# Constant products in the expert stage's waits, results added one instruction at a time, one normalisation moved to ScalarE, and Newton chains of 11 operations

## The reference

```python
h = take(weight, x)                                  # token rows
h = h + linear_attention(layernorm(h))               # layer 0: relu(q), relu(k), groups of 512 tokens
h = h + expert_choice_ffn(layernorm(h))              # layer 0: 32 experts, each takes its 512 best tokens
h = h + causal_attention(layernorm(h))               # layer 1: 64 batches of 256 tokens, 8 heads of width 128
h = h + top2_ffn(layernorm(h))                       # layer 1: 8 experts, 2 for each token

def expert_choice_ffn(xf):                           # 16384 x 128
    S = softmax(xf @ W_router + b_router)
    G, idx = top_k(S.T, 512)                         # for each of 32 experts
    up = silu(xf[idx] @ W_up[group] + b_up)          # 341 wide
    out = G * (up @ W_down + b_down)
    return zeros.at[idx].add(out)
```

## Time and profile before

| | us |
|---|---|
| median of 3 runs (2581.69 to 2586.2) | 2584.89 |
| the profiled execution | 2591.4 |
| its span in the profile | 2589.7 |

### The profile page before, as it was taken

How to read it: one execution, slowest core, us unless ns; L and a number is a source line. 1 busy time by engine, 2 the same in 40 slices (tenths; PEclk the granted TensorE clock), 3 DMA queues, 4 the chain that set the end, 5 groups by cost and what they waited for, 6 DMA issues and landing times.

```text
span 2589.7 us, 59542 instructions
## 1 busy us (share of the span) xinstructions
PE 2264.2 (87%) x16671; PEld 1982.4 (77%) x16687; DVE 1896.1 (73%) x8436; ACT 1686.8 (65%) x5272; POOL 1473.5 (57%) x1870
## 2 busy tenths in 40 slices
PE   4988978576776899999999999999999999999954
PEld 4877756344443788988888899999998888988854
DVE  4877756656663688888888887887788888888622
ACT  3777744122222777777777788888887777777643
POOL 6444200467766578788888864444444665366553
PEclk9999989789888999999999999999999999999987
DMA  2666630244444611111111146566546776476687
GB/s 73 212 229 205 222 121 1 83 138 142 140 135 131 138 42 42 46 45 49 47 44 46 43 135 171 161 163 172 165 134 187 222 217 198 128 227 196 174 254 241
DMA packets 343687, 357.42 MB, mean 138 GB/s; under 512 B 36491, under 2 KB 285931, under 8 KB 343360
## 3 DMA queue, kind: packets, MB, share of 16 engines
q1 hardware_dynamic: 305856, 265.69, 35.9%
q0 software_dynamic: 34048, 80.03, 9.5%
q10 hardware_dynamic: 3456, 7.89, 1.0%
HBM read 211.02 MB, written 136.67 MB: 134 GB/s over the span
## 4 chain that ended last, share of the span: by engine, by line
PE 54%; DVE 22%; DMA 7%; issue 7%; POOL 4%; ACT 3%; SPq 2%; ACTq 0%; DVEq 0%; POOLq 0%
PE bank L2068 6%; PE bank L2158 6%; PE bank L2144 5%; PE bank L2079 4%; PE bank L2024 4%; PE bank L2111 4%; PE bank L2119 3%; PE bank L2067 3%; PE bank L2091 3%; PE bank L2093 3%; PE bank L2092 3%; PE bank L2037 3%; DVE pr_place L1577 2%; DMA rows<-table,idx 2%; DVE nmax L1557 2%
## 5 line engine op out<-in xcount | busy, mean ns | idle before, releaser
L881 POOL DMA_INDIRECT zbuf<-pc,kb x248 | 250.4, 1010 | 272.8 <-DVE pc L1742 221.9
L866 POOL DMA_INDIRECT spread_rows<-kb,pos x256 | 256.1, 1000 | 171.3 <-DVE pc L1742 81.0
L1081 ACT ACTIVATE pr_place<-bank,nmax 128x128 f32<-128x128 f32 x512 | 188.5, 368 | 223.6 <-DVE nmax L1557 223.5
L2068 PE MATMUL bank<-xT,gT 128*128 128x256 f32 x1024 | 307.4, 382 | 0.0
L1577 DVE COPY pr_place<-bank 128x384 f32<-128x384 f32 x512 | 280.6, 548 | 9.2 <-PE bank L2079 7.8
L2158 PE MATMUL bank<-wvo_part,x_part 128*128 128x512 f32 x768 | 269.3, 459 | 0.0
L2079 PE MATMUL bank<-ident,pr_place 128*128 128x128 f32 x1536 | 252.3, 273 | 17.2 <-DVE pr_place L1577 17.0
L1556 DVE TENSOR_REDUCE nmax<-bank 128x1 f32<-128x128 f32 x512 | 142.9, 279 | 169.1 <-PE bank L2068 167.2
L1091 ACT ACTIVATE bank<-causal 128x384 f32<-128x384 f32 x512 | 253.4, 495 | 19.5 <-PE bank L2202 3.3
L2079 PEld LDWEIGHTS bank<-ident,pr_place 128*128 128x128 f32 x1536 | 195.4, 140 | 87.1 <-DVE pr_place L1570 22.1
L2144 PE MATMUL bank<-x_part,wqk_part 128*128 128x256 f32 x1536 | 245.6, 296 | 1.2 <-DVE x_part L1684 1.2
(11 more groups left out here) (338 smaller groups left out, 6472.9 us busy)
## 6 DMA issues: line engine op xcount, KB each, us to landing
pa<-bundle SPq DMA_DIRECT2D x198, 321.0 KB
table<-rows SPq DMA_DIRECT2D x96, 576.0 KB, 7.0
rows<-table SPq DMA_DIRECT2D x192, 128.0 KB
wu_more<-bundle SPq DMA_DIRECT2D x66, 321.0 KB
junk<-zbuf SPq DMA_DIRECT2D x32, 512.0 KB
kb<-spread_rows SPq DMA_DIRECT2D x248, 65.0 KB
h3buf<-h SPq DMA_DIRECT2D x64, 128.0 KB
kb<-kb SPq DMA_DIRECT2D x32, 256.0 KB
```

The costliest lines, as they stand in the source:

```text
L866: pool.indirect_dma_start(out=spread_rows, out_offset=bass.IndirectOffsetOnAxis(ap=pos[:, k, j:j + 1], axis=0), in_=xr4s[g % 2][:, k, j], ...
L2068: pe.matmul(s2[:, P:3 * P], g[:, P:2 * P], xT3[:, p], start=False, stop=True, skip_group_check=True)\
```

## The change

Four edits. (1) `turn_rows` begins with six constant products into bank 0, ahead of its wait for the gather, and after it two more into bank 3 stand ahead of the wait for `xeT`. (2) `add_rows` and `add_residual` take one tile at a time: `adding` puts one instruction near the start of GpSimd's slot and one at its end, so that the two sums of a result take four slots and not two. (3) `prep_norm` is two ScalarE instructions (`Identity` with a scale and a bias for each row) in slot 4, behind the copy of `gT`; VectorE makes the bias (`prep_shift`, a 128x2 instruction, slot 3). A semaphore that this needed was freed (`b1_ready`: SP's `make_bundle` now waits for `xeT_ready`, which comes later on the same engine). (4) `inv_sqrt` has 11 operations: the factor -0.5 goes into the first, and the constant of the second is adapted. Every one of them now waits for the one before; earlier the third waited for nothing.

```diff
+            def stay_warm(b, times):
+                for _ in range(times):
+                    pe.matmul(bank[b][:, :], slot16[:, 0:P], slot16[:], start=True, stop=True)
+
             def turn_rows(e):
+                stay_warm(0, 6)
                 pe.wait_ge(xe_in[e % 2], 64 * (e // 2 + 1))
...
                     turn_rows(e)
+                    stay_warm(3, 2)
                     pe.wait_ge(xeT_ready, e + 1)
...
-            def add_rows(c):
-                pool.wait_ge(z_in[c % 2], 32 * (c // 2 + 1))
...
+            def adding(u, later):
+                for d in range(2):
+                    if u - 2 - d in RESULT_AT and u - d < U:
+                        add_rows(RESULT_AT[u - 2 - d], 2 * d + later)
+                    if u - 4 - d in RESULT_AT and u - 2 - d < U:
+                        add_residual(RESULT_AT[u - 4 - d], 2 * d + later)
...
+                adding(u, 0)
                 if gated(i - 2) and i <= NG and 1 <= h <= TG:
...
-                if u - 2 in RESULT_AT and u < U:
-                    add_rows(RESULT_AT[u - 2])
-                if u - 3 in RESULT_AT and u <= U:
-                    add_residual(RESULT_AT[u - 3])
+                adding(u, 1)
...
+            def prep_norm(n, p):
+                act.wait_ge(prep_ready, n + 1)
+                if n > 0:
+                    act.wait_ge(xT3_mm, n)
+                for j in range(2):
+                    ins = act.activation(xn3[:, j], hx[:, p, j], ACT.Identity, bias=nm3[:, j:j + 1], scale=r3[:, 0, j:j + 1])
+                ins.then_inc(xn3_ready, 1)
...
+                        if h == 4 and n + 1 < NB:
+                            prep_norm(n + 1, 1 - p)
                         if h == 5 and n + 1 < NB:
                             turned(n + 1, 1 - p)
...
-                if k != 2:
-                    steps.wait()
+                steps.wait()
                 if k == 0:
-                    ins = dve.tensor_scalar(h, v, EPS, None, ALU.add)
+                    ins = dve.tensor_scalar(h, v, EPS, -0.5, ALU.add, ALU.mult)
...
-                elif k == 2:
-                    ins = dve.tensor_scalar(h, h, -0.5, None, ALU.mult)
+                elif k % 3 == 2:
+                    ins = dve.tensor_tensor(t, y, y, ALU.mult)
...
-            def prep_norm(n, p):
+            def prep_shift(n):
                 prep_now["steps"].wait()
-                    ins = dve.tensor_scalar(xn3[:, j], hx[:, p, j], mv3[:, j, 0:1], r3[:, 0, j:j + 1], ALU.subtract, ALU.mult)
+                dve.scalar_tensor_tensor(out=nm3[:], in0=mv3[:, :, 0], scalar=-1.0, in1=r3[:, 0], op0=ALU.mult, op1=ALU.mult)\
+                    .then_inc(prep_ready, 1)
```

More of the change, by code:

```diff
@@ L1 @@
 from contextlib import ExitStack
+from functools import partial
 import concourse.bass as bass
@@ L243, in lm_tower @@
         r3 = sb("r3", [P, 3, 2])
+        nm3 = sb("nm3", [P, 2])
         xn3 = sb("xn3", [P, 2, C])
@@ L451, in lm_tower @@
         consts4 = sem("consts4")
-        b1_ready = sem("b1_ready")
+        prep_ready = sem("prep_ready")
         d_step = sem("d_step")
@@ L640, in make_bundle @@
                 sp.wait_ge(w_c, 16 * (12 + NK))
-                sp.wait_ge(b1_ready, 1)
+                sp.wait_ge(xeT_ready, 1)
                 place = bundle.rearrange("x p c -> p x c")
@@ L883, in give_unit, with add_rows, add_residual @@
                     bounds_check=2 * NTOK - 1, oob_is_err=False).then_inc(z_out[t % YR], 16)
-            def add_rows(c):
-                pool.wait_ge(z_in[c % 2], 32 * (c // 2 + 1))
[L887 to L897, removed]
+            def add_rows(c, j):
+                if j == 0:
+                    pool.wait_ge(z_in[c % 2], 32 * (c // 2 + 1))
+                    if c >= 2:
+                        pool.wait_ge(out_done[c % 2], 16 * (c // 2))
+                ins = pool.tensor_tensor(res[:, c % 2, j], zx[:, c % 2, j, 0:C], zx[:, c % 2, j, C:2 * C], ALU.add)
+                if j == TG - 1:
+                    ins.then_inc(res_step, 1)
+            def add_residual(c, j):
+                if j == 0:
+                    pool.wait_ge(res_step, c + 1)
+                ins = pool.tensor_tensor(res[:, c % 2, j], res[:, c % 2, j], h3x[:, c % 2, j], ALU.add)
+                if j == TG - 1:
+                    ins.then_inc(res_ready, 1)
             def normalise(u, h):
@@ L1040, in _ @@
                     act.wait_ge(bup_mm, 2)
-                    act.activation(b1T[:].rearrange("p x k -> p k x"), bank[2][:, 0:2 * E1].rearrange("p (k x) -> p k x", k=2), ACT.Copy).then_inc(b1_ready, 1)
+                    act.activation(b1T[:].rearrange("p x k -> p k x"), bank[2][:, 0:2 * E1].rearrange("p (k x) -> p k x", k=2), ACT.Copy)
             act.wait_ge(bup_ready, 2)
@@ L1098, in _ @@
                 set_mask(u)
+            prep_norm(0, 0)
             turned(0, 0)
@@ L1205, in _ @@
             assert bias.n == BIAS_STEPS
[L1207 removed]
+            ROOT = 11
             def inv_sqrt(k, steps, v, y, t, h):
[L1211 to L1212 removed]
+                steps.wait()
                 if k == 0:
[L1214 removed]
+                    ins = dve.tensor_scalar(h, v, EPS, -0.5, ALU.add, ALU.mult)
                 elif k == 1:
[L1216 to L1218 removed]
+                    ins = dve.tensor_scalar(y.bitcast(I32), h.bitcast(I32), -0.5, float(0x5F3759DF - (1 << 30) - (1 << 22)), ALU.mult, ALU.add)
+                elif k % 3 == 2:
+                    ins = dve.tensor_tensor(t, y, y, ALU.mult)
                 elif k % 3 == 0:
[L1220 to L1221 removed]
                     ins = dve.tensor_tensor(t, t, h, ALU.mult)
@@ L1539, in prep_stats, with prep_root @@
                 n_.wait()
-            def prep_root(k):
+            def prep_root(n, k):
+                if k == 0 and n > 0:
+                    dve.wait_ge(xn3_ready, n)
                 if k < ROOT:
                     inv_sqrt(k, prep_now["steps"], mv3[:, :, 1], r3[:, 0], r3[:, 1], r3[:, 2])
-            def prep_norm(n, p):
+            def prep_shift(n):
                 prep_now["steps"].wait()
-                if not first(n):
-                    dve.wait_ge(xT3_mm, n)
-                for j in range(2):
-                    ins = dve.tensor_scalar(xn3[:, j], hx[:, p, j], mv3[:, j, 0:1], r3[:, 0, j:j + 1], ALU.subtract, ALU.mult)
-                ins.then_inc(xn3_ready, 1)
+                dve.scalar_tensor_tensor(out=nm3[:], in0=mv3[:, :, 0], scalar=-1.0, in1=r3[:, 0], op0=ALU.mult, op1=ALU.mult)\
+                    .then_inc(prep_ready, 1)
             def maxima(u, h):
@@ L1690, in _ @@
             for k in range(ROOT):
-                prep_root(k)
-            prep_norm(0, 0)
+                prep_root(0, k)
+            prep_shift(0)
             assert prep_now["steps"].n == PREP
@@ L1762, in slots @@
                         if h in (1, 2, 3) and n + 1 < NB:
-                            root = [prep_root, 5 * (h - 1), 1, 1]
+                            root = [partial(prep_root, n + 1), 5 * (h - 1), 1, 1]
                         elif p == 0 and h in (6, 7) and gated(i - 1):
@@ L1799, in slots @@
                         if h == 3 and n + 1 < NB:
-                            prep_norm(n + 1, 1 - p)
+                            prep_shift(n + 1)
                         if h == 6 and n + 1 < NB:
```

## The result

| | us |
|---|---|
| median of 5 runs (2564.35 to 2569.22) | 2568.23 |
| before beside it, median of 5 runs | 2586.2 |
| ratio, 95% interval | 0.9927 [0.9909, 0.9945] |
| span of the profiled execution (before 2589.7) | 2566.5 |

A forecast was written before the change was run, and what follows sets the result against it. Late gathers and TensorE's lowered clock were taken to bound the expert stage, TensorE itself 1500 to 1900 us. Terms -23.4 - 9 + 3 + 1 = -28.4 us gave 2556.5 us, range 2545 to 2573.

The forecast's parts named there:

- Constant products: Expert stage: eight products per expert fill TensorE's waits and hold its clock; -23.4 us, bounds 0 and -25.
- waits for the gather stay under 1 us: Expert stage, profile after: TensorE's waits for each expert's gathered rows were to be shorter than 1 us.
- I take 0: First expert: six products at half speed cost 2.6 us and may give back 1.8 + 0.9; net put at 0.
- Rival (a): Expert stage: the clock holds only in part, so half of the 23.4 us comes; 2568 us, chance 0.15.
- (e): Expert stage: products run, but the clock falls during the rest of the gather wait; 2580 us, chance 0.04.
- Spread sums: Late layer 1: shorter runs of GpSimd's sums cut TensorE's waits for VectorE's copy and clock falls; -9 us, bounds 0 and -14.
- The step that sized a wait by GpSimd's run: Late layer 1: VectorE waits out GpSimd's unbroken run of sums; six 2.54 us, four 1.7, two 0.85.
- Rival (b): Late layer 1: the lock goes by single instructions, the gate's list makes the waits; -9 falls away, 2565.5 us, chance 0.10.
- ScalarE: Layer 1 batches: normalisation moved to ScalarE delays TensorE's transposes 0.05 to 0.2 us; +3 us, range 0 to +12.
- (c): Layer 1: ScalarE carries the moved work half visibly, 0.3 us for 63 batches; +16, 2572 us, chance 0.08.
- (d): TensorE's full stretch: ScalarE's 0.87 us per batch lie fully ahead of the exponentials; slower, 2608 us, chance 0.03.
- Newton chains: Inverse roots: less VectorE issue, but one operation moves ahead of the copy in the gate's first slot; +1 us, -2 to +4.

## Why the prediction was right, and where it was off

**Constant products: right.** -23.4 was forecast; with this edit alone batch 0 starts 23.3 us earlier (844.93 to 821.66), and the time falls by 22 (19 to 26). The clock holds from the second expert on, GpSimd is the bound at 10.2 us for each expert, and six products end within the cycle. The sign that waits for the gather stay under 1 us was missed: they go up to 1.83. The first expert's products cost 2.6 us (transposes at 480.79, not 478.19) and its first scatter came 0.2 late (488.82, 489.02), so "I take 0" held. Rival (a) did not come: the clock holds in spite of these waits. Nor did (e). With the whole change batch 0 gains 20.9, not 23.3: the rest is the start of layer 1, which is back by batch 2.

**Spread sums: right in size, wrong in make-up.** -9 was forecast and -9.0 measured (-8 us alone). The two parts were put as two thirds of 8.9 us of waits and of 4.5 of clock. That is 6 us for the waits and 3 for the clock. The clock gave at most 3.4, as forecast. The waits are the term that was mis-sized: those for the copy did not get less, 17.0 us in 20 places against 16.7 in 16 before. They are each shorter, 2.23 at most, but there are more of them, and TensorE's whole idle time fell by 2.8 and not by 6. The 2.8 that are left lie in TensorE's instructions at the upper clock and were in no term, so that the size came out right is in part luck. That two of four falls went because the waits ahead of them got shorter is not shown: in the kernel with ScalarE's edit alone, which has waits up to 3.34 us, there are two falls as well. The signs put for this edit were missed, the first two narrowly: a wait of 2.23 us and not under 2, an L1567 of 1.92 and not 1.9, and two stretches at the lower clock where none was to be. The step that sized a wait by GpSimd's run held: longest L1567 2.5 and 2.9 with six, 1.7 and 1.9 with four, 1.2 to 1.3 with three or two, 0.75 with round trips everywhere. Rival (b), the lock by single instructions, needs an answer in two halves. With round trips VectorE gets in after one of GpSimd's instructions. Without them it does not, although they are single instructions just as well; it came in 0.3 us before the end of the last one of the run. So what the Trainium skill says (SBUF — State Buffer, SBUF: two separate sides), that the lock lasts for one whole instruction, the runs agree with where GpSimd has none ready behind it (0.75 at most). Where it has, the further reading that VectorE is next does not hold (2.5).

**ScalarE: right.** +3 forecast, with +12 as the far end; 2.4 + 0.7 = +3.1 alone by batch 47, and +4 in time (+1 to +7). The delay is 0.1 us at the transposes of every batch from 2 to 31, and only 0.11 for a pair of them, so that half of it is swallowed; I had put 0.05 to 0.2 for each batch. The exponentials of that slot start 0.09 us late, and not 0.2; (c) and (d) did not come.

**Newton chains: the term that was mis-sized.** +1 forecast, of it +2 for the operation moved ahead of the copy, -0.9 and -1 for the issue that falls away. Measured alone: 2.8 + 1.1 = +3.9 by batch 47, and +4 in time (+1 to +8). The first part is right (0.20 for a pair). The issue that falls away, -0.9, shows nowhere between batches 2 and 47; whether layer 0 gained its -1 can't be told from a profile (batch 0 starts at 843.7, and at 843.0 in the kernel with ScalarE's edit alone). And the 16 batches from 31 to 47, whose eight pairs I had put at nothing, pay it too.

**Sum.** By the profiles it is 23.2 us and not 28.4: Newton chains and ScalarE +7.1 and not +4, and the tail +2.0 and not 0. By the runs it is 19. The forecast time, 2556.5, subtracted the same 28.4 from the median of three runs, 2584.89; the medians of later comparisons, 2586.2 and 2588.0, lie nearer the profiled execution. So the measured 2568.2 is 11.7 above it, inside the range but outside the likeliest case's own 2548 to 2565: 5.2 of that by the terms and 6.5 by the starting point. That it is just what rival (a) gave is chance, since that rival's mechanism did not come.

**What the forecast did not see** is that its sign holds for an occasion. No rival named the case in which the eight products do not pay; kernels with all eight took 37 to 49 us more than before there. From the one profile none could be priced.

## What to carry to other kernels

Look at what an engine does during a wait as well as how long it waits: 2.7 us of idling cost TensorE another 2.7 in clock, and work without use in its place gave 22 us where the wait had room for it. On the other occasion each of the four kernels with it was slower than before, by 37 to 49 us. Where GpSimd computes beside VectorE, read its instructions' runs: a wait on its own last result between two of them, at about 0.1 us each, gave about 25 us beside the products (0.9819 against 0.9914), where their spreading gave 8; it has not been measured alone on the first occasion. An operation saved in a chain is worth nothing if another takes its place ahead of the copy that TensorE waits for: look at the order around that copy first.

## What the runs showed of the hardware

- VectorE's instruction on 128x128 that takes 0.27 us alone took 2.5 us beside six of GpSimd's without a break and at most 0.75 with a semaphore round trip between them. The issue of an indirect transfer can hold it as well: here, with products and round trips, L1572 ends at 1919.93, just behind GpSimd's instruction (1919.88). It does not always: of 119 that start during such an issue in this trace, 56 end before it does, nearly all after 0.27 or 0.28 us.

```profile
1918.92 0.96 POOL L882 DMA_INDIRECT zbuf<-pc,kb  x1 [2.10 <-DVE pc L1747]
...
1919.27 0.66 DVE L1572 TENSOR_SCALAR pr_place<-pr_place,rinv 128x128 f32<-128x128 f32 x1
```

- The same program took 2588 us on two chips and 2750 on two others, and a change that gave 0.7% beside a before of 2586 cost 1.8% beside one of 2750. What makes the two differ is open. A gain of under 2% that fills waits should be measured on more than one chip.
